# Edge rows of a graph layer: two chunks per load instead of one

## The chip, the cores and the metric

One Trainium2 chip, one core. The metric is the device time of one launch in microseconds (us). The kernel is one program with five instruction streams: TensorE (PE, with PEld for its weight loads), VectorE (DVE), ScalarE (ACT), GpSimd (POOL) and the queue of SyncE (SP), which does nothing here but wait and issue DMAs.

## The reference, cut to what matters

6,250 nodes of 128 features, 100,000 edges sorted by `dst`. Two graph layers follow one another.

```
# layer 0: messages by a small MLP, summed at dst, then node update and layer norm
h = silu(concat(x[src], x[dst], radial(edge_weight)) @ Wm1 + bm1)
h = silu(h @ Wm2 + bm2);  messages = h @ Wm3 + bm3
x = layernorm(x + node_mlp(x, segment_sum(messages, dst)))
# layer 1: every edge's 128 attributes (edge_attr_128) are read once
xt   = logmap0(x)
att  = sigmoid(concat(xt[src], xt[dst], edge_attr) @ att_w.T + att_b)
sup  = xt + segment_sum(xt[src]*att, src) + segment_mean(edge_attr, src) + segment_mean(edge_attr, dst)
x = layernorm(x + proj(expmap0(sup)))
```

## The kernel before, in words

The edges are cut into 196 chunks of 512 (the last one overlaps its neighbour, so that it is full). All loops run over chunks in "ticks" that are written out: in each tick every engine does one step of several chunks at different depths.

**Layer 0** (ticks t = -6 to 218, `layer_*`). POOL gathers the source rows of a chunk with four indirect DMAs (L1069), PE, ACT and DVE form the messages (L1293 to L1333).

**Rows.** Layer 1 reads each chunk's attributes as a row buffer `row[i % 8]` of 128 partitions x 4 x 131 words; there are eight. The row tick r is t - 190, so rows begin while layer 0 ends; from r = 29 on the functions are `rest_*`. For row chunk i:

- SP loads it in tick i - 3: `row_load`, L890 to L897, one DMA of 256 KB. From i = 8 on it first waits until the four scatters of chunk i - 8 have landed (semaphore `sc`) and PE has read that buffer (`rp`).
- DVE (`rows_dve`) builds a one-hot (L978), multiplies the row with the attention weights (L981), and from chunk 62 on multiplies looked-up terms (L987) and copies one column (L989); ACT (`rows_act`) sums them (L944 up to chunk 61, L949 and L952 after it) and writes two columns of the row.
- POOL (`rows_pool`) scatters the row with four indirect DMAs (L933) into a table in HBM, sorted by source block.
- PE (`rows_pe`, L1010) adds the row into the sum at `dst`.

**Looks.** From chunk 62 on DVE needs a table look-up for the chunk: SP loads three small pieces in tick i - 4 (`look_load`, L1437, the last one is `bval`), DVE compares them (L1534) in tick i - 2, PE multiplies (L1639).

**Units.** The scattered table is read back in 206 units (`unit_load`, L1423), each one a one-hot on DVE (L1543), up to six matmuls on PE (L1660) and an addition on DVE (L1568). A unit of a group may only be loaded once the last chunk of that group has been scattered; seven buffers are used in turn.

In a tick of `rest_sp` the order on SP's queue is fixed: the row load of chunk r + 3, the look of chunk r + 4, then the units of tick r + 2. Whatever SP waits for, all behind it waits too.

```
for r in RTICKS:
    batch_sp(e, R0 + r)
    ...
    rows_sp(e, r)
    if C1 <= r + 4 < M:
        look_load(r + 4)
    for k in UTICK.get(r + 2, []):
        if unit_at(k) is not None:
            unit_load(unit_at(k))
```

**The end.** After the last rows (tick 195) PE runs the units of ticks 196 to 198, then transposes the sum at `dst` (L1648, with ACT L1492 between), then the last 25 units, and DVE and ACT finish the nodes.

Of the kernel before, what the change touches and what calls it, by code (L numbers as in the profile page):

```python
# [2 lines left out]
N, E, H = 6250, 100000, 128  # L3
P = 128
NB = 49
NP = NB * P
ME = 512
M = 196
# [9 lines left out]
NE, NGP, NOD = 8, 6, 4  # L18
# [3 lines left out]
RC = H + 3  # L22
# [10 lines left out]
def edge0(m):  # L33
    return min(m * ME, LASTB)
# [155 lines left out]
def gnn_kernel(nc, A, out):  # L190
# [6 lines left out]
    V, S, T, G, SP = nc.vector, nc.scalar, nc.tensor, nc.gpsimd, nc.sync  # L197
# [3 lines left out]
    with ctx:  # L201
# [7 lines left out]
        def region(name, size):  # L209
            return Region(sb(name, [P, size]), size)  # L210

        def take(reg, shape, dt=f32):
            n = 1
            for k in shape:
                n *= k
            return reg.take(shape, None if dt == f32 else dt, n // 2 if dt == bf16 else n)

        s = {n: ctx.enter_context(nc.semaphore(n)) for n in PRO + LAYER + NODES + ROWS + REST}
# [49 lines left out]
        ring = region("ring", 17408)  # L268
# [448 lines left out]
        od2 = [take(ring, [4, W]) for _ in range(NO2)]  # L717
        prod = [take(ring, [4, H + W]) for _ in range(NPR)]
        bwin = [take(ring, [W]) for _ in range(NWN)]
        row = [take(ring, [4, RC]) for _ in range(NE)]  # L720
        assert ring.off >= STAGE + 13 * 4 * H
        pat = take(ring, [FILL * RC])
        lgs = [take(ring, [4]) for _ in range(2)]
# [19 lines left out]
        def small_free(e, t):  # L743

            e.wait_ge(s["acch"], min(M, t - 8))
            e.wait_ge(s["tot"], min(M, t - 2))
            e.wait_ge(s["cnt"], min(M, t - 2))
            e.wait_ge(s["acce"], min(M, t - R0 - 2))
# [137 lines left out]
        def look(e, name, i):  # L886

            if i >= C1:
                e.wait_ge(lk[name], M + i - C1 + 1)

        def row_load(e, i):
            e0 = edge0(i)
            if i >= NE:
                e.wait_ge(s[f"sc{i % NE}"], 64 * (i // NE))
                e.wait_ge(s["rp"], i - NE + 1)
            SP.dma_start(row[i % NE][:, :, 0:H], A["edge_attr_128"][e0:e0 + ME, :].rearrange(
                "(s p) f -> p s f", p=P)).then_inc(s[f"ea{i % NE}"], 16)  # L897

        def window_load(e, i):
            e.wait_ge(s["abw"], 48)  # L900
            e.wait_ge(s["dm"], i - NWN + 1)
            SP.dma_start(bwin[i % NWN], btab[bass.ds(window(SP, i), W)].rearrange("(o w) -> o w", o=1).to_broadcast(
                [P, W])).then_inc(s[f"wn{i % NWN}"], 16)

        def rows_loaded(e, i):

            for j in range(NE):
                if i >= j:
                    e.wait_ge(s[f"ea{j}"], 16 * ((i - j) // NE + 1))

# [8 lines left out]
                    e.wait_ge(s[f"sc{j}"], 64 * ((i - j) // NE + 1))  # L919

        def rows_sp(e, r):
            if 0 <= r + 3 < M:
                row_load(e, r + 3)
            if 0 <= r + 3 < C1:
                window_load(e, r + 3)
# [10 lines left out]

        def rows_act(e, i):
            if 0 <= i < M:
                e.wait_ge(s[f"ea{i % NE}"], 16 * (i // NE + 1))
                S.copy(row[i % NE][:, :, RC - 1:RC], lo["s"][:, :, i:i + 1])  # L940
                e.wait_ge(s["dm"], i + 1)
                if i < C1:
                    for n in range(4):
                        k = S.activation(prod[i % NPR][:, n, :], prod[i % NPR][:, n, :], ACT.Identity,  # L944
                                         accum_out=row[i % NE][:, n, H:H + 1])
                    k.then_inc(s["lb"], 1)
                else:
                    for n in range(4):
                        k = S.activation(prl[i % NPR][:, n, :], prl[i % NPR][:, n, :], ACT.Identity, accum_out=lgs[i % 2][:, n:n + 1])  # L949
                    k.then_inc(lk["dot"], 1)  # L950
                    look(e, "dot", i)
                    S.activation(row[i % NE][:, :, H:H + 1], lgs[i % 2].rearrange("p (s o) -> p s o", o=1), ACT.Sigmoid,  # L952
                                 bias=attb[:, :]).then_inc(s["lb"], 1)

        def row_bank(i):

            return small_bank(R0 + i + 1) if i < RL - 1 else banks[(3, 7, 4)[i % 3]]
# [14 lines left out]
        def rows_dve(e, r):  # L972
            i = r
            if 0 <= i < M:
                v = prod[i % NPR] if i < C1 else prl[i % NPR]
                e.wait_ge(s["lb"], i - NPR + 1)
                e.wait_ge(s["rp"], i - NO2 + 1)
                V.tensor_tensor(od2[i % NO2], iotap[:, 0:W].rearrange("p (o b) -> p o b", o=1).to_broadcast([P, 4, W]),  # L978
                                rel[:, :, i:i + 1].to_broadcast([P, 4, W]), ALU.is_equal).then_inc(s["odr"], 1)
                e.wait_ge(s[f"ea{i % NE}"], 16 * (i // NE + 1))  # L980
                V.tensor_tensor(v[:, :, 0:H], row[i % NE][:, :, 0:H], attp.rearrange("p (o f) -> p o f", o=1).to_broadcast(  # L981
                    [P, 4, H]), ALU.mult)
                if i >= C1:
                    bk = banks[(1, 2)[i % 2]][:, :].rearrange("p (s m) -> p s m", s=4)
                    look(e, "prd", i)
                    for n in range(4):
                        V.scalar_tensor_tensor(out=v[:, n, H:H + NM], in0=iota[:, 0:NM], scalar=srcm[:, n, i:i + 1], in1=bk[:, n, 0:NM],  # L987
                                               op0=ALU.is_equal, op1=ALU.mult)
                    V.tensor_copy(v[:, :, H + NM:H + NM + 1], bk[:, :, NM:NM + 1]).then_inc(s["dm"], 1)  # L989
                    return  # L990
                e.wait_ge(s[f"wn{i % NWN}"], 16 * (i // NWN + 1))
                e.wait_ge(s["dm"], i)
                V.tensor_copy(bwinp, bwin[i % NWN]).then_inc(s["bwp"], 1)
                e.wait_ge(s["odr"], i + 1)
                e.wait_ge(s["bwp"], i + 1)
                V.tensor_tensor(v[:, :, H:H + W], od2[i % NO2], bwinp.rearrange("p (o b) -> p o b", o=1).to_broadcast([P, 4, W]),  # L996
                                ALU.mult).then_inc(s["dm"], 1)

        def rows_pe(e, r, first):
            i = r - 1  # L1000
            if 0 <= i < M:
                bk = row_bank(i)
                if i < RL - 1:
                    small_free(e, R0 + r)
                else:
                    e.wait_ge(s["acce"], max(i - 2, RL - 1))
                e.wait_ge(s["odr"], i + 1)
                e.wait_ge(s[f"ea{i % NE}"], 16 * (i // NE + 1))
                for n in range(4):
                    k = T.matmul(bk[:, 256:256 + W], row[i % NE][:, n, 0:H], od2[i % NO2][:, n, :], start=(first and n == 0),  # L1010
                                 stop=(n == 3), skip_group_check=True)
                k.then_inc(s["rp"], 1)
# [62 lines left out]
        def layer_act(e):  # L1075
            settled(e)
            for t in TICKS:
# [32 lines left out]
                if j is not None:  # L1110
                    e.wait_ge(s["nz"], j + 1)
                    e.wait_ge(s["n1"], j)
                    S.activation(nu[:, 0:n, :], nz[:, 0:n, :], ACT.Silu).then_inc(s["nu"], 1)
                batch_act(e, t)
                rows_act(e, t - R0)

        def ranks_ready(e):
# [47 lines left out]
        def layer_dve(e):  # L1165
# [4 lines left out]
            for t in TICKS:  # L1170
# [101 lines left out]
                if j is not None:  # L1272
# [6 lines left out]
                    k.then_inc(s["nz"], 1)  # L1279
                batch_dve(e, c, t)  # L1280
                rows_dve(e, t - R0)

        def layer_pe(e):
# [131 lines left out]
        def rest_sp(e):  # L1415
# [23 lines left out]
            for r in RTICKS:  # L1439
                batch_sp(e, R0 + r)  # L1440
                if r == TAB:
                    e.wait_ge(s["abw"], 80)
                    e.wait_ge(s["pat"], 3)
                    for v in tw:
                        SP.dma_start(v[0:NQ, 0:NM], atab[0:N].rearrange("(q m) -> q m", m=NM)).then_inc(s["abb"], 16)
# [6 lines that stand above are left out]
# [243 lines left out]
        def early_done(e):  # L1695

            slots_done(e, RE - 1)
            rows_loaded(e, RL + 2)
            windows_loaded(e, RL + 2)
            e.wait_ge(s["rp"], RL - 1)  # L1700
            e.wait_ge(s["acce"], RL - 2)
            e.wait_ge(s["lb"], RL)
            e.wait_ge(s["odr"], RL)
            e.wait_ge(s["abw"], 48)
            e.wait_ge(s["zacc"], ZACC)
            e.wait_ge(s["mvs"], 2 * NB)
            e.wait_ge(s["zf"], 16 * len(FILLS))
# [413 lines left out]
```

## Time and profile before

| | us |
|---|---|
| three runs | 2115.41, 2115.46, 2117.05 (median 2115.46) |
| the profiled execution | 2115.82 |
| its span | 2114.0 |
| POOL busy | 1501.2 (71%) |
| DVE busy | 1693.4 (80%) |
| PE busy | 1550.7 (73%) |
| ACT busy | 1358.8 (64%) |

Busy times are sums over the whole span; what counts is which engine never waits in a stage, and which wait ends last. Of the 2115.82 us the span is 2114.0, so 1.8 us lie around it.

### The profile page before, as it was taken

The numbers are of one execution on the slowest core, as the hardware profiler recorded it, in microseconds if no ns is written. First come the engines' busy times: TensorE is split into PE (matmuls) and PEld (weight loads), VectorE is DVE, ScalarE is ACT, GpSimd is POOL, SyncE is SP. The second block draws the span as 40 slices with busy tenths as digits, with TensorE's granted clock in tenths as the row PEclk, the third lists the DMA queues.
The fourth block names the chain that finished last, engine by engine and source line by source line (L and its number), as shares of the span: only waits on it lengthen the run. The fifth ranks groups of instructions, "written<-read, shape, count | busy, mean of one in ns | idle before, by whom it ended". The sixth has DMA issues, their size and how long they took to land.

```text
span 2114.0 us, 41847 instructions
## 1 busy us (share of the span) xinstructions
PE 1550.7 (73%) x11127; PEld 1334.6 (63%) x11225; DVE 1693.4 (80%) x5532; ACT 1358.8 (64%) x3965; POOL 1501.2 (71%) x1572
## 2 busy tenths in 40 slices
PE   7787888888888887887874334676778877778850
PEld 7566666666676666666664334666677877778740
DVE  6877788788888888888766543899998788888887
ACT  4887787777787877987654533688884434434424
POOL 3777777777777777777777777777777777777700
PEclk9899999999999999999965555699999899989985
DMA  9577767676653434335464344788877778888822
GB/s 243 150 181 152 178 168 173 155 174 161 160 122 100 106 105 106 100 95 128 114 174 111 112 119 121 203 231 234 230 214 224 215 225 228 233 232 241 264 72 61
DMA packets 345860, 349.60 MB, mean 165 GB/s; under 512 B 67792, under 2 KB 273610, under 8 KB 345617
## 3 DMA queue, kind: packets, MB, share of 16 engines
q1 hardware_dynamic: 292193, 241.07, 44.5%
q0 software_dynamic: 50176, 104.07, 16.7%
q10 hardware_dynamic: 3248, 1.71, 0.3%
q8 instruction: 94, 1.54, 0.3%
q14 instruction: 149, 1.22, 0.2%
HBM read 249.43 MB, written 94.46 MB: 163 GB/s over the span
## 4 chain that ended last, share of the span: by engine, by line
DVE 36%; POOL 28%; issue 14%; DVEq 7%; PE 7%; ACT 3%; DMA 2%; SPq 1%; POOLq 0%; ACTq 0%
POOL gtab L933 20%; POOL ra L1069 9%; DVEq L758 7%; DVE ring L1193 4%; DVE ring L1203 3%; DVE rt L987 2%; DVE ring L1208 2%; DVE bank L1217 2%; DVE ring L1198 2%; DVE ring L1214 2%; PE bank L1660 2%; DVE ring L1195 2%; DVE ring L1543 1%; DVE ra L1178 1%; DVE ring L978 1%
## 5 line engine op out<-in xcount | busy, mean ns | idle before, releaser
L1069 POOL DMA_INDIRECT ra<-ptab,gis x784 | 746.8, 953 | 271.8 <-issue 225.8
L933 POOL DMA_INDIRECT gtab<-ring,idx x784 | 754.2, 962 | 239.1 <-issue 236.4
L949 ACT ACTIVATE rt<-rt 128x254 f32<-128x254 f32 x536 | 215.3, 403 | 291.2 <-DVE rt L989 291.2
L1010 PE MATMUL bank<-ring 128*128 128x78 f32 x1568 | 261.1, 323 | 127.5 <-DMA ring<-in_edge_attr 88.4
L1010 PEld LDWEIGHTS bank<-ring 128*128 128x128 f32 x1568 | 247.8, 241 | 137.9 <-issue 109.2
L1293 PEld LDWEIGHTS bank<-ring 128*128 128x128 f32 x1568 | 197.9, 195 | 143.7 <-DVE ra L1178 127.3
L1293 PE MATMUL bank<-ring 128*128 128x78 f32 x1568 | 209.7, 278 | 62.5 <-DVE ring L1185 56.0
L1660 PE MATMUL bank<-ring 128*128 128x130 f32 x1374 | 195.1, 293 | 57.1 <-DVE ra L1568 41.3
L1639 PE MATMUL bank<-rt 128*128 128x126 f32 x1072 | 165.8, 304 | 80.8 <-DVE rt L989 66.7
L1320 PE MATMUL bank<-wm,ring 128*128 128x128 f32 x1568 | 215.9, 283 | 10.8 <-ACT ring L1102 4.8
L1320 PEld LDWEIGHTS bank<-wm,ring 128*128 128x128 f32 x1568 | 213.5, 198 | 11.5 <-ACT ring L1102 5.6
L1660 PEld LDWEIGHTS bank<-ring 128*128 128x128 f32 x1374 | 174.6, 201 | 67.4 <-DVE ra L1568 47.7
L1639 PEld LDWEIGHTS bank<-rt 128*128 128x128 f32 x1072 | 149.2, 215 | 90.9 <-issue 90.9
L1082 ACT ACTIVATE ring<-bank 128x512 f32<-128x512 f32 x196 | 116.2, 593 | 137.8 <-PE bank L1320 136.1
L944 ACT ACTIVATE ring<-ring 128x206 f32<-128x206 f32 x248 | 89.6, 363 | 127.0 <-DVE ring L996 126.8
L1329 PE MATMUL bank<-cst,ra 128*128 128x128 f32 x784 | 127.1, 287 | 50.6 <-DMA ra<-ptab,gis 50.2
L1178 DVE TENSOR_TENSOR ra<-ra,bank 128x78 f32 x196 | 46.3, 236 | 131.8 <-issue 124.0
L1333 PE MATMUL bank<-ra,ring 128*128 128x512 f32 x264 | 148.0, 643 | 4.6 <-DVE ra L1252 3.8
L987 DVE SCALAR_TENSOR_TENSOR rt<-cst,rt,bank 128x125 f32<-128x125 f32 x536 | 147.3, 336 | 0.0
L1102 ACT ACTIVATE ring<-bank,bcol 128x512 f32<-128x512 f32 x196 | 134.7, 687 | 13.2 <-PE bank L1333 9.7
L1534 DVE TENSOR_SCALAR rt<-rt,cst 128x512 f32<-128x512 bf16 x134 | 67.4, 503 | 85.4 <-DMA rt<-bval 83.7
L1193 DVE TENSOR_TENSOR ring<-bank,lo_d 128x512 bf16<-128x512 f32 x196 | 133.9, 683 | 0.0
(274 smaller groups left out, 3587.0 us busy)
## 6 DMA issues: line engine op xcount, KB each, us to landing
ring<-in_edge_attr SPq DMA_DIRECT2D x196, 256.0 KB, 3.7
ring<-gtab SPq DMA_DIRECT2D x89, 393.0 KB
gtab<-ring SPq DMA_DIRECT2D x41, 687.8 KB
ra<-in_edge_weight SPq DMA_DIRECT2D x132, 128.0 KB
ring<-gtab SPq DMA_DIRECT2D x49, 327.5 KB
ring<-reld SPq DMA_DIRECT2D x196, 78.0 KB
ring<-gtab SPq DMA_DIRECT2D x49, 262.0 KB
ra<-ptab,gis POOLq DMA_INDIRECT x784
```

The costliest lines, as they stand in the source:

```text
L758: return eng.value_load(baser[0:1, m:m + 1], min_val=0, max_val=TOP)
L933: G.indirect_dma_start(out=gtab[group_of(i)][:, :], out_offset=bass.IndirectOffsetOnAxis(ap=idx[:, n, i:i + 1], axis=0), in_=row[i % NE][: ...
L949: k = S.activation(prl[i % NPR][:, n, :], prl[i % NPR][:, n, :], ACT.Identity, accum_out=lgs[i % 2][:, n:n + 1])
L987: V.scalar_tensor_tensor(out=v[:, n, H:H + NM], in0=iota[:, 0:NM], scalar=srcm[:, n, i:i + 1], in1=bk[:, n, 0:NM], op0=ALU.is_equal, op1=A ...
L1010: k = T.matmul(bk[:, 256:256 + W], row[i % NE][:, n, 0:H], od2[i % NO2][:, n, :], start=(first and n == 0), stop=(n == 3), skip_group_chec ...
L1069: G.indirect_dma_start(out=gp[i % NGP][:, n, :], out_offset=None, in_=ptab[:, :], in_offset=bass.IndirectOffsetOnAxis(ap=gis[:, n, i:i + 1 ...
L1193: V.tensor_tensor(l, iotap.rearrange("p (o b) -> p o b", o=1).to_broadcast([P, 4, P]), lo["d"][:, :, i:i + 1].to_broadcast([P, 4, P]), ALU ...
L1293: k = T.matmul(small_bank(t)[:, 0:W], val[i % NVAL][:, n, :], ohd[i % NOD][:, n, :], start=(n == 0), stop=(n == 3), skip_group_check=True)
L1320: k = T.matmul(bk[:, n * P:(n + 1) * P], h1[i % 2][:, n * P:(n + 1) * P], wm2[:, :], start=False, stop=True, skip_group_check=True)
L1333: T.matmul(bk[:, :], qw[i % NQW], rad[i % NRD], start=False, stop=True, skip_group_check=True).then_inc(s["h1p"], 1)
L1639: k = T.matmul(banks[(1, 2)[i % 2]][:, n * P:n * P + NM + 1], lkf[i % 2][:, n * P:(n + 1) * P], tw[i % NLK][:, 0:NM + 1], start=(n == 0), ...
L1660: k = T.matmul(bk[:, j * (H + 2):(j + 1) * (H + 2)], coh1[(u - 4) % NCO][:, j * nk + n, :], ct[(u - 4) % NCT][:, j * nk + n, 0:H + 2], sta ...
```

## The change

Row buffers are taken in pairs: `duo[k]` holds 8 x 131 words per partition, and `row[2k]`, `row[2k + 1]` are its halves, so the layout in memory is the same. `row_load` is called in every second tick, for the even chunk i, and loads chunks i and i + 1 with one DMA of 512 KB on the semaphore of the even buffer. It waits for the scatters of chunks i - 8 and i - 7 and for PE's reading of chunk i - 7. The last two chunks (194 and 195) are loaded in the same call by two DMAs, each on its own semaphore. All who read a row wait through `row_here`. The number of buffers (eight), their users, the looks, the units and the scatters are as before.

```diff
-        row = [take(ring, [4, RC]) for _ in range(NE)]
+        duo = [take(ring, [8, RC]) for _ in range(NE // 2)]
+        row = [duo[i // 2][:, 4 * (i % 2):4 * (i % 2) + 4, :] for i in range(NE)]
...
         def row_load(e, i):
-            e0 = edge0(i)
             if i >= NE:
                 e.wait_ge(s[f"sc{i % NE}"], 64 * (i // NE))
-                e.wait_ge(s["rp"], i - NE + 1)
-            SP.dma_start(row[i % NE][:, :, 0:H], A["edge_attr_128"][e0:e0 + ME, :].rearrange(
-                "(s p) f -> p s f", p=P)).then_inc(s[f"ea{i % NE}"], 16)
+                e.wait_ge(s[f"sc{i % NE + 1}"], 64 * (i // NE))
+                e.wait_ge(s["rp"], i - NE + 2)
+            if i < M - 2:
+                SP.dma_start(duo[i % NE // 2][:, :, 0:H], A["edge_attr_128"][i * ME:(i + 2) * ME, :].rearrange(
+                    "(s p) f -> p s f", p=P)).then_inc(s[f"ea{i % NE}"], 16)
+            else:
+                for v in (i, i + 1):
+                    e0 = edge0(v)
+                    SP.dma_start(row[v % NE][:, :, 0:H], A["edge_attr_128"][e0:e0 + ME, :].rearrange(
+                        "(s p) f -> p s f", p=P)).then_inc(s[f"ea{v % NE}"], 16)
+
+        def row_here(e, i):
+
+            if i < M - 1:
+                e.wait_ge(s[f"ea{i % NE // 2 * 2}"], 16 * (i // NE + 1))
+            else:
+                e.wait_ge(s[f"ea{i % NE}"], 16)
...
         def rows_sp(e, r):
-            if 0 <= r + 3 < M:
+            if 0 <= r + 3 < M and (r + 3) % 2 == 0:
                 row_load(e, r + 3)
...
         def rows_act(e, i):
             if 0 <= i < M:
-                e.wait_ge(s[f"ea{i % NE}"], 16 * (i // NE + 1))
+                row_here(e, i)
```

`rows_dve` and `rows_pe` get the same line as `rows_act`.

## Rows read from the trace of the kernel before

**Rows 1.** The page: busy time by engine; the two costliest groups

```profile
PE 1550.7 (73%) x11127; PEld 1334.6 (63%) x11225; DVE 1693.4 (80%) x5532; ACT 1358.8 (64%) x3965; POOL 1501.2 (71%) x1572
...
L1069 POOL DMA_INDIRECT ra<-ptab,gis x784 | 746.8, 953 | 271.8 <-issue 225.8
L933 POOL DMA_INDIRECT gtab<-ring,idx x784 | 754.2, 962 | 239.1 <-issue 236.4
```

**Rows 2.** Line L933: ns min/median/max, first and last start; its idle time by releaser

```profile
L933 POOL DMA_INDIRECT gtab<-ring,idx x784: 954/958/1250, 1019.4 to 2011.4; - x196
...
  issue: 236.4, 775
  ACT ring L944: 2.1, 7
  ACT ring L952: 0.6, 2
```

**Rows 3.** Chain that ended last, from 1940 us on: start, us, what

```profile
1955.37 6.09 DMA gtab<-ring,idx
...
1964.44 0.41 SPq L896
...
1966.53 4.08 DMA rt<-bval
1970.64 0.48 DVE rt L1534
...
1985.91 4.59 PE bank L1660 x24
...
1991.35 9.75 PE bank L1660 x84
...
2001.63 11.46 ACT ra L1492 x44
...
2013.46 9.44 PE bank L1660 x84
...
2026.31 12.17 PE bank L1660 x78
```

**Rows 4.** Timeline of SP's queue, 1960 to 1990 us

```profile
1970.44 0.38 SPq L896 DMA_DIRECT2D ring<-in_edge_attr  x1
...
1972.50 0.32 SPq L1437 DMA_DIRECT2D rt<-bval  x1
...
1974.27 0.40 SPq L896 DMA_DIRECT2D ring<-in_edge_attr  x1
```

**Rows 5.** Timeline of DVE, 1969 to 1990 us

```profile
1975.66 0.48 DVE L1534 TENSOR_SCALAR rt<-rt,cst 128x512 f32<-128x512 bf16 x1
...
1982.89 0.68 DVE L981 TENSOR_TENSOR rt<-ring,bank 128x512 f32<-128x512 f32 x1
```

**Rows 6.** Waits: engine line, waited for, us in total, times, longest

```profile
SPq L896 <- DMA gtab<-ring,idx: 359.6, 163, 5.2
```

**Rows 7.** Line L896: issue ns, waiters, landing us min/median/max

```profile
L896 SPq DMA_DIRECT2D ring<-in_edge_attr x196: 378/389/1642, 979.9 to 1974.3; - x196
...
  PE bank L1010: 88.4, 29
  DVE ring L981: 39.9, 30
  ACT ring L940: 24.0, 22
...
DMA to landing us min/median/max: 2.7/3.7/6.6
```

**Rows 8.** Windows with counts: L952 and L933 to chunk 108, L944 and L933 to chunk 8

```profile
0.00:1555.90 1555.90, 15.18 (x47) 0.88 0.59 153
...
0.00:1566.10 1566.10, 415.04 (x432) 0.88 0.59 154
...
0.00:1056.90 1056.90, 13.72 (x72) 0.96 0.58 143
...
0.00:1059.80 1059.80, 30.77 (x32) 0.96 0.58 144
```

**Rows 9.** Windows: us, busy PE PEld DVE ACT POOL, granted clock, DMA share, GB/s

```profile
1700.00:1975.00 275.00, 216.29 (x1693) 208.49 (x1693) 231.65 (x666) 114.37 (x549) 208.83 (x218) 0.93 0.81 233
...
1985.00:1991.00 6.00, 5.09 (x31) 5.09 (x31) 4.53 (x9) 1.70 (x9) 4.68 (x5) 0.72 1.09 367
1991.00:2001.00 10.00, 10.00 (x89) 9.87 (x88) 9.13 (x16) 0.00 (x0) 7.66 (x8) 1.00 0.96 298
```

**Rows 10.** Timeline of the end: PE L1660 at two moments

```profile
1971.10 1.55 PE L1660 MATMUL bank<-ring,pos 128*128 128x130 f32 x12
...
1985.91 2.97 PE L1660 MATMUL bank<-ring,gis 128*128 128x130 f32 x12 [2.02 <-DVE ra L1568]
```

More of the change, by code:

```diff
@@ L905, in rows_loaded @@
         def rows_loaded(e, i):
-            for j in range(NE):
+            for j in range(0, NE, 2):
                 if i >= j:
@@ L979, in rows_dve @@
                                 rel[:, :, i:i + 1].to_broadcast([P, 4, W]), ALU.is_equal).then_inc(s["odr"], 1)
-                e.wait_ge(s[f"ea{i % NE}"], 16 * (i // NE + 1))
+                row_here(e, i)
                 V.tensor_tensor(v[:, :, 0:H], row[i % NE][:, :, 0:H], attp.rearrange("p (o f) -> p o f", o=1).to_broadcast(
@@ L1007, in rows_pe @@
                 e.wait_ge(s["odr"], i + 1)
-                e.wait_ge(s[f"ea{i % NE}"], 16 * (i // NE + 1))
+                row_here(e, i)
                 for n in range(4):
```

## The prediction

> **What bounds the kernel now.** I read the page first. By busy time DVE leads with 80% and POOL has 71% [rows 1], but the idle time of POOL's two groups is almost all "issue": a short gap after each indirect DMA. The lines of L933 say it outright: 784 scatters from 1019.4 to 2011.4 us, idle 236.4 us by issue (775 times, 0.305 us each) and 2.7 us by anything else [rows 2]. So POOL, once it scatters, never waits: 992.0 us between first and last start, over 783 intervals, is 1.267 us each, 5.07 us a chunk. Nothing in DVE, PE, ACT or SP can bring its last scatter earlier, and a delay elsewhere costs POOL nothing as long as each row is ready in time.
>
> The second view is the chain that ended last, read at its end [rows 3]. The reader is to see that it leaves POOL at 1955, 57 us before POOL's last scatter is issued. It goes: a scatter lands, SP issues a row load and the look behind it (L896, then `bval`), DVE L1534 starts at 1970.64 when `bval` has landed, DVE works through the last rows, PE runs units (L1660), ACT and PE transpose (11.46 us of ACT), PE runs the rest until 2038.5, and DVE and ACT finish. From 1985.9 on every piece follows the one before it. So two things set the time: POOL's pace, and **when the last rows get through DVE**, which hangs on SP's queue, which hangs on POOL's scatters. The third view, the waits of SP's queue, confirms the link: L896 waited 359.6 us in 163 waits for scatters to land [rows 6]. Row loads are not issued when there is time, but when a buffer comes free.
>
> **The change part by part.**
>
> 1. *97 row DMAs fewer.* Each took SP 0.389 us to issue [rows 7], 38 us in all, out of a queue that spends 359.6 us waiting in front of that very line. Worth nothing while SP waits. The readers' waits for odd rows fall away too; a few hundredths each on engines that are not POOL. Nothing.
>
> 2. *The row itself comes later.* PE, DVE and ACT waited 88.4, 39.9 and 24.0 us for rows [rows 7], none of it POOL. An even row now waits for chunk i - 7 instead of i - 8: 5.07 us. Its load is 512 KB; from the 2.7 to 6.6 us of the 256 KB one [rows 7] I take a microsecond more for the second half: 256 KB at 233 to 298 GB/s [rows 9] are 1.1 to 0.9 us, nothing at the least. What hides it is POOL's lead time, and it is thinnest at two places. At chunk 8, ACT has finished the row at 1056.9 (72 instructions of L944, eight a chunk, nine chunks) and POOL starts it just after 1059.8 (32 scatters done) [rows 8]: 2.9 us. But that row was loaded 25 us before DVE used it (eight rows were free at the start), so 6 us more in the load don't reach it. At chunk 108 (the 47th L952, done by 1555.9; POOL comes after 1566.1, 432 scatters done) it is 10 us [rows 8]. There the whole DVE phase moves with the loads: minus 6 to 7.5 us, 3 to 4 us are left. POOL goes on unhindered: cost 0.
>
> 3. *The look behind the row load.* This is the step that costs. In an odd tick SP now stands in front of the pair until chunk r - 4 has landed, where it used to need only r - 5; the look of chunk r + 4 and the units of tick r + 2 are queued behind it. In even ticks it waits for no scatter. In the steady part that moves DVE by a chunk against POOL and is covered by the same lead time. At the end it isn't. The last look, for chunk 195, is issued in tick 191, which is odd. Before, its row load (chunk 194) went out at 1970.44 and `bval` at 1972.50, 2.06 us behind [rows 4]; L1534 ran at 1975.66 [rows 5]. Afterwards SP waits for what the load of chunk 195 waited for, 1974.27 [rows 4]: 3.83 us later. It then issues two row DMAs where one stood: 0.45 us. `bval` goes out at 1974.27 + 2.06 + 0.45 = 1976.78. With the 4.08 us that `bval` took on the chain [rows 3] L1534 starts at 1980.86 instead of 1975.66: **5.2 us later**. Bounds: with the 3.16 us between `bval`'s issue and L1534 of that tick (1972.50 to 1975.66), 4.3 us. At POOL's mean pace of 5.07 us instead of the 3.83 of this execution, and with the extra microsecond of a second row ahead of it in the rings, 5.07 + 0.45 + 0.92 + 1.0 = 7.4 us. I take the value in between, as its terms are the nearest rows.
>
> The tick before does not undo this: the look of chunk 194 goes out in an even tick with no wait, so DVE is through with its tick by 1979 and stands at the one of chunk 195.
>
> 4. *From there to the end.* DVE needs 7.2 us from that L1534 to L981 of the last row (1982.89 [rows 5]); then everything is in a row as before [rows 3]. PE was busy for 10.00 of 10.00 us from 1991 to 2001 [rows 9], so nothing there swallows a late start. The last scatter, issued at 2011.4 [rows 2], is needed by the last units after 2013.46 [rows 3]; it was there in time and still is. So the 5.2 us arrive whole.
>
> Sum: 0 + 0 + 5.2 us on the profiled execution's 2115.82 us, 2121.0; that execution lies 0.36 us above the median of 2115.46, so 2120.7.
>
> At one point the Trainium skill speaks against this sum. The rows say that no transfer's size is waited for by POOL [rows 2]. "DMA: Bandwidth & Descriptors", section "Anatomy of one DMA", gives a DMA a fixed part of about 2.0 us beside bytes / 436 GB/s, and its rules for authors ask for larger ones; an estimate by it is 3.2 us for a pair where two loads take 5.2 us, which would make the change a gain. No run here shows it, and it is a rival below.
>
> **The rivals.**
>
> *The shift is swallowed (not slower).* Place: PE between 1985.9 and 1991. There PE was granted 0.72 of its clock on average against 1.00 after it [rows 9], and twelve matmuls of L1660 took 2.97 us where they took 1.55 before [rows 10], after PE had stood idle for 2.02 us. It is the lower of its two levels, 1.2 GHz, for part of the stretch. If PE falls idle elsewhere in the new order and runs this stretch at 2.4 GHz, two such groups give back up to 2.8 us: 2120.7 - 2.8 = 2117.9. With the lower bound of step 3, 4.3 - 2.8 = 1.5 us, 2117.0. It decides from 1 us given back. For it: the idle gap of 2.02 us hangs on DVE. Against: PE will stand idle longer before 1981 than it did, which speaks for the lower clock.
>
> *POOL runs dry near chunk 108.* If the phase moves by more than the 10 us of lead [rows 8], POOL waits for ACT, and its end moves by what is missing. Should the pair cost DVE two chunks of pace (10.1 us) and the upper terms of step 3 (0.45 + 0.92 + 1.0) besides, 12.5 us, then 2.5 us are missing; POOL's scatters are late by that, and the last look with them: 2120.7 + 2.5 = 2123.2, or 2125.4 with the upper bound of step 3. For it: DVE is busiest there. Against: step 2 leaves 3 to 4 us.
>
> *The DMA queues were what held DVE (faster).* If the fixed part of a load counted, fewer loads would bring rows and looks sooner; half of DVE's 39.9 us of waits for rows [rows 7] would go, 20 us: 2095. By the page above this is the rule's outcome. For it: the DMA engines are 81% busy from 1700 to 1975 [rows 9]. Against: POOL waits for none of it, and the last look cannot go out before chunk 187's scatter lands.
>
> **How the numbers follow.** A measurement of this kernel tells 0.2%, 4.2 us, from no change: slower begins at 2119.7. Forecast (4.3 to 7.4 us, 2119.8 to 2122.9): 0.57. Swallowed, 2115.5 to 2119.6: 0.32. POOL dry, 2123 to 2126: 0.05. Faster, near 2095: 0.06. Slower 0.62, same 0.32, faster 0.06. The range holds the forecast with its bounds, the swallowed case and most of the dry one: 2115.0 to 2126.0; left out are the faster case and the edges.
>
> **What would show it.** Right: L933 again from about 1019 to 2011 us without waits; 99 row DMAs in L896; L1534 of the last look 4.3 to 6 us later, waiting for `bval`; transposes starting near 2006 instead of 2001. Step 2 wrong: POOL idle behind L944 or L952. Step 4 wrong: the last L981 late, but L1660 after the transposes not. The forecast as a whole is wrong if the last L1534 is not late, or if POOL's first or last scatter has moved.

## The result and the profile after

The changed kernel takes 2125.5 us (2124.95 to 2127.94, 5 runs) against 2116.09 us of the kernel before: 1.0045 times as long (95% interval 1.0034 to 1.0057), 9.4 us. A second measurement of the same kernel (e9 below) gave 1.0034 (1.0022 to 1.0047), 7.2 us. It is slower, as forecast, and by more than the 5.2 us of the forecast; 2125.5 lies just inside the range (2115.0 to 2126.0) and above the forecast's own bounds (2119.8 to 2122.9). The profiled execution took 2127.94 us, the longest of its five, so the differences of this one trace run some 2 us above those of the medians.

POOL's scatters after the change (line L947, the view of [rows 2]):

```profile
L947 POOL DMA_INDIRECT gtab<-ring,idx x784: 952/958/1251, 1018.8 to 2014.7; - x196
its engine sat idle before it (us, times) until:
  issue: 226.8, 742
  ACT ring L966: 12.8, 38
  ACT ring L958: 1.7, 4
```

The reader is to see two things. The last scatter starts 3.3 us later, at 2014.7 instead of 2011.4. (The first one started 0.6 us earlier, but the second started at 1020.7 in both traces, so nothing was lost by that.) And ACT's L966, the last step of a row, is now named 38 times instead of twice. POOL's timeline around chunk 106 shows what that is, with the ACT line that released it:

```profile
1556.39 0.96 POOL L947 DMA_INDIRECT gtab<-ring,idx  x1 [0.30 <-issue]
1558.86 1.00 POOL L947 DMA_INDIRECT gtab<-ring,idx  x1 [1.50 <-ACT ring L966]
```
```profile
1557.80 0.30 ACT L966 ACTIVATE ring<-ring,attb 128x4 f32<-128x4 f32 x1
```

Instead of the usual 0.30 us POOL stood for 1.50 us, because the row was ready only at 1558.10. At chunk 8 it stood 0.81 us for L958:

```profile
1060.42 0.95 POOL L947 DMA_INDIRECT gtab<-ring,idx  x1 [0.81 <-ACT ring L958]
```

These two stops are 1.2 and 0.5 us of the 3.3. The other 1.6 us are in the scatters themselves, which were busy for more of the time than the 754.2 us of before [rows 1], and no wait goes with that:

```profile
L947 POOL DMA_INDIRECT gtab<-ring,idx x784 | 755.8, 964 | 241.4 <-issue 226.8
```

The end of the chain that ended last (the view of [rows 3]), as far as it stands in SP's queue and behind it:

```profile
1974.32 6.15 DMA gtab<-ring,idx
1980.53 0.38 SPq L903
1980.95 0.52 SPq L903
...
1983.83 3.69 DMA rt<-bval
1987.54 0.58 DVE rt L1548
...
1997.88 4.49 PE bank L1674 x24
...
2003.33 9.75 PE bank L1674 x84
...
2013.61 11.49 ACT ra L1506 x44
...
2025.48 9.44 PE bank L1674 x84
...
2038.33 12.18 PE bank L1674 x78
```

From the PE pieces on it is the same chain, link for link, 12 us later: the PE piece of 24 stands at 1997.88 (before 1985.91), the transposes' ACT piece at 2013.61 (before 2001.63), the last PE piece at 2038.33 (before 2026.31). Ahead of them it differs: before, the `bval` on the chain was that of chunk 194 [rows 3], here it is that of the last look. DVE's timeline, the last look and the last row:

```profile
1987.54 0.58 DVE L1548 TENSOR_SCALAR rt<-rt,cst 128x512 f32<-128x512 bf16 x1 [4.10 <-DMA rt<-bval]
...
1994.86 0.68 DVE L995 TENSOR_TENSOR rt<-ring,bank 128x512 f32<-128x512 f32 x1
```

DVE stood 4.10 us for `bval`; before it hadn't stood there at all [rows 5]. From the last row to the end of the span it is 2126.0 - 1994.86 = 131.1 us, and before it was 2114.0 - 1982.89 = 131.1 us [rows 5]. In seven of the traces below it is 130.9 to 131.1 us again, in e1 and e9 129.3, in e6 and e11 133.9 and 133.4. So in most traces what delays the last row delays the end by as much.

So one figure weighs each kernel below, **how far the last row runs ahead of POOL**: from L981 of chunk 195 (its line is another one in some kernels) to the start of the last scatter. Before it is 2011.4 - 1982.89 = 28.5 us [rows 2, 5], after it is 2014.7 - 1994.86 = 19.8 us. Of the 12 us of this trace 3.3 are POOL's and 8.7 the shrunken lead. Each such figure comes from one execution.

### The profile page after: what moved, and what is told of

Its sections match the earlier page's. It is cut to its first block, busy times and chain, and to the rows that moved or that the text cites. A ratio compares the mean times of both kernels' runs of the same rounds, so it can differ in the third digit from the quotient of the medians.

```text
span 2126.0 us, 41648 instructions
## 1 busy us (share of the span) xinstructions
PE 1547.9 (73%) x11127; PEld 1332.0 (63%) x11225; DVE 1688.9 (79%) x5532; ACT 1358.2 (64%) x3965; POOL 1503.3 (71%) x1572
## 4 chain that ended last, share of the span: by engine, by line
DVE 36%; POOL 23%; issue 14%; DMA 7%; DVEq 7%; PE 7%; ACT 4%; SPq 2%; POOLq 0%; ACTq 0%
POOL gtab L947 14%; POOL ra L1083 8%; DVEq L759 7%; DVE ring L1207 4%; DVE rt L1001 3%; DVE ring L1217 3%; DMA gtab<-ring,idx 3%; DMA rt<-bval 3%; DVE ring L1222 2%; DVE bank L1231 2%; PE bank L1674 2%; DVE ring L1212 2%; DVE ring L1228 2%; DVE ring L1209 2%; DVE rt L995 1%
## 5 line engine op out<-in xcount | busy, mean ns | idle before, releaser
L947 POOL DMA_INDIRECT gtab<-ring,idx x784 | 755.8, 964 | 241.4 <-issue 226.8
L958 ACT ACTIVATE ring<-ring 128x206 f32<-128x206 f32 x248 | 89.7, 363 | 93.6 <-DVE ring L1010 93.6
L1116 ACT ACTIVATE ring<-bank,bcol 128x512 f32<-128x512 f32 x196 | 134.8, 688 | 11.9 <-PE bank L1347 8.5
L1548 DVE TENSOR_SCALAR rt<-rt,cst 128x512 f32<-128x512 bf16 x134 | 66.8, 499 | 94.5 <-DMA rt<-bval 94.1
```

Source lines behind the costliest of these rows:

```text
L947: G.indirect_dma_start(out=gtab[group_of(i)][:, :], out_offset=bass.IndirectOffsetOnAxis(ap=idx[:, n, i:i + 1], axis=0), in_=row[i % NE][: ...
```

## The experiments

Theory: SP's queue makes look and units wait behind the pair, which costs at the end, and POOL's lead near chunks 8 and 106 is used up. Rival: the rows themselves come too late, or the transfer of 512 KB costs. All ratios are to the kernel before, measured beside it on the same chip, and the microseconds named with a ratio are worked out from it. e1 to e4 ran on one chip, where the kernel before stood at 2116.2 us, e5 to e8 and e9 to e11 on another, where it stood at 2120.1 and 2119.6, so only ratios are compared.

**e1, pairs up to chunk 167, and e2, pairs from chunk 168 on.**

```diff
+        def paired(i):
+            return 0 <= i < 168          # e2: 168 <= i < 194; e8: 64 <= i < 120
...
+            if paired(i):                # one load for i and i + 1, as in the change
+                if i % 2:
+                    return
+            else:                        # one load for i, as before the change
```

> Pairs up to chunk 167, single loads from 168 on. Theory (the late look at the end costs 5 to 7 us, POOL running dry near chunks 8 and 106 costs 2 to 3): the end is as before, POOL's last scatter stays 2 to 3 us late, so 2117.5 to 2119.5. Rival, only the end counts: 2116 (nothing left). Rival, all of it is POOL being late or slower scatter landings everywhere: 2121 or more.

> Single loads up to chunk 167, pairs from 168 on (194 and 195 singly, as before the change). Theory: the end's share alone, 5 to 7 us, POOL's scatters end at 2012 as before: 2121 to 2123. Rival, all from POOL: 2116. If both shares add up, this run's difference and that of e1 give the whole, 9 us.

e1: 2117.81 us, 1.0005 (0.9996 to 1.0014). e2: 2121.19 us, 1.0026 (1.0016 to 1.0035), 5.5 us. The end's share is real and the larger one; the pairs of the first 168 chunks cost 1.1 us, and their interval includes no change at all. Together the two make 6.6 us, against 7.2 to 9.4 for the whole. e2's queue shows something that the forecast had not in it (SP's timeline, where L908 is a pair and L915 a single load, then DVE's):

```profile
1965.33 0.40 SPq L908 DMA_DIRECT2D ring<-in_edge_attr  x1
...
1971.19 0.42 SPq L915 DMA_DIRECT2D ring<-in_edge_attr  x1
...
1973.42 0.32 SPq L1460 DMA_DIRECT2D rt<-bval  x1
```
```profile
1980.07 0.48 DVE L1557 TENSOR_SCALAR rt<-rt,cst 128x512 f32<-128x512 bf16 x1
...
1987.30 0.68 DVE L1004 TENSOR_TENSOR rt<-ring,bank 128x512 f32<-128x512 f32 x1
```

Chunks 194 and 195 are single loads there and wait singly, and the last `bval` went out at 1973.42, not late. Yet DVE came to the last look at 1980.07, with no wait in front of it: it was still busy with the ticks that the pair before (L908) had held up. In those ticks it had waited for `bval` in every second one (2.25 us at 1950.84, 1.01 at 1960.77, 0.79 at 1971.23). The delay isn't made by the last pair alone; it is DVE's whole phase, set by each pair in turn.

**e3, the waits of the change with two loads of 256 KB.**

```diff
-            if i < M - 2:
-                SP.dma_start(duo[i % NE // 2][:, :, 0:H], ...).then_inc(s[f"ea{i % NE}"], 16)
-            else:
-                for v in (i, i + 1):
+            for v in (i, i + 1):
...
         def row_here(e, i):
+            e.wait_ge(s[f"ea{i % NE}"], 16 * (i // NE + 1))
```

> The waits of the change, but each pair as two loads of 256 KB on two semaphores. Theory: the wait costs, not the size: 2124 to 2127, as after the change (0.45 us more of issue in front of the look). Rival, the 512 KB transfer itself costs (it lands later or delays scatters and looks): back by half or more, 2116 to 2120.

2123.09 us, 1.0032 (1.0020 to 1.0045). This is just under the 2124 to 2127 expected; most of the loss is there without a single large transfer. Against the first 1.0045 it left room for a share of the size, so it was repeated as e10.

**e4, the look ahead of the row load.** **e5, look and units ahead of it.**

```diff
-                rows_sp(e, r)
                 if C1 <= r + 4 < M:
                     look_load(r + 4)
+                rows_sp(e, r)            # e4: here
                 for k in UTICK.get(r + 2, []):
                     if unit_at(k) is not None:
                         unit_load(unit_at(k))
+                rows_sp(e, r)            # e5, e6: here instead
```

> The change, with the look issued ahead of the row load in SP's queue from tick 29 on. Theory: what the pair delays is the look behind it; freed of it, DVE is only held by the rows, which come 6 to 8 us earlier than DVE used them: 2111 to 2117. Rival, the late rows or the bigger transfer cost: 2121 to 2126.

e4: 2121.31 us, 1.0023 (1.0014 to 1.0032). The theory in this form missed: the loss did not go. It is smaller than that of the change (1.0045 and 1.0034), but the interval overlaps with that of e9. The chain and DVE's timeline of e4 say why:

```profile
1978.28 5.50 DMA ring<-gtab
```
```profile
1983.80 0.96 DVE L1557 TENSOR_TENSOR ring<-bank,ring 128x768 f32<-128x768 f32 x1 [2.21 <-DMA ring<-gtab]
```

The look (L1548 in this kernel) no longer waits behind the pair, and the unit load, next behind it, does. So the next kernel freed both.

> The change, with look and units both ahead of the row load in SP's queue from tick 29 on. Theory now: all that is queued behind the pair's wait comes late, and with the look freed it was the unit load (DVE waited 2.2 us for it in tick 193 of e4); with both freed DVE is held by its own work: 2112 to 2117. Rival, the late rows themselves or their size: 2121 as in e4.

e5: 2119.35 us, 0.9998 (0.9989 to 1.0007): the loss is gone, with every pair, its late rows and its 512 KB transfers in place. In its trace, which is of its fastest execution (2116.03 us), the last look and last row on DVE stand where they stood before the change (1975.66 and 1982.89 [rows 5]):

```profile
1975.74 0.51 DVE L1548 TENSOR_SCALAR rt<-rt,cst 128x512 f32<-128x512 bf16 x1
...
1983.00 0.68 DVE L995 TENSOR_TENSOR rt<-ring,bank 128x512 f32<-128x512 f32 x1
```

POOL's scatters run from 1019.1 to 2011.1 us in it, 992.0 us, as in the kernel before.

**e6, the same order with single loads.** The edit is e5's on the kernel before.

> The kernel before, with the same order on SP's queue: look, units, row load. Theory: the wait for a scatter stood in front of both before the change too, so this is faster than before, by 1 to 4 us: 2112 to 2115; and the pairs of e5 cost little against it, 0 to 3 us. Rival, DVE at the end is held by the rows: 2116, no change.

2117.17 us, 0.9987 (0.9978 to 0.9997). It was repeated as e11. This kernel, and not the one before, has the same order as e5: between the two, pairs cost 2.2 us by the medians (2119.35 against 2117.17), and the two intervals overlap.

**e7, single loads on time, look and units late.**

```diff
                 rows_sp(e, r)
+                if (r + 3) % 2 == 0 and r + 3 < M:
+                    e.wait_ge(s[f"sc{(r + 4) % NE}"], 64 * ((r + 4) // NE))
                 if C1 <= r + 4 < M:
                     look_load(r + 4)
```

> The kernel before with its single row loads at their old times, but with a wait for the scatter of chunk r - 4 put between row load and look in odd ticks of the rest stage. Theory: look and units are as late as with pairs, rows are not: the most of the change's loss, 2121 to 2125, with the last look 5 us late or more and POOL's lead near chunk 106 used up. Rival, the late or bigger row load is the cause: 2116.

2124.33 us, 1.0023 (1.0014 to 1.0032), 4.9 us. This is the counterpart to e5: the row loads and their waits are those of the kernel before, and the loss is of the size of the end's share (e2). Its chain, then DVE's timeline:

```profile
1974.81 5.11 DMA gtab<-ring,idx
...
1981.54 4.23 DMA rt<-bval
```
```profile
1985.80 0.49 DVE L1536 TENSOR_SCALAR rt<-rt,cst 128x512 f32<-128x512 bf16 x1 [1.70 <-DMA rt<-bval]
...
1993.03 0.69 DVE L981 TENSOR_TENSOR rt<-ring,bank 128x512 f32<-128x512 f32 x1
```

One part of the expectation missed. The row was ready 2.1 us ahead of POOL's scatter at chunk 106, not at the least value of 0.76 us, so POOL didn't run dry, and this kernel lacks that share. It also stays below the 7.2 us of the whole.

**e8, pairs for chunks 64 to 119 alone** (the edit of e1).

> Pairs for chunks 64 to 119 alone. Theory: POOL's lead near chunk 106 goes from 5.9 to its least value, 0.8 us, POOL's last scatter is 0 to 1.5 us later, the ramp is as before; the phase is back by the end, so 2116 to 2118. Rival, the loss of e1 came from the ramp: lead of 2 us or more left, 2116.

2120.64 us, 1.0001 (0.9992 to 1.0010). POOL's timeline has the same stop, before the same scatter of chunk 106:

```profile
1561.57 1.00 POOL L956 DMA_INDIRECT gtab<-ring,idx  x1 [1.50 <-ACT ring L975]
```

So the pairs of this stretch make POOL run dry, as the theory said; that it costs time can't be told from the runs of this kernel. In e1, whose pairs cover this stretch too, the row of chunk 106 was just in time (0.8 us ahead) and POOL made no stop before the same scatter:

```profile
1556.74 0.96 POOL L956 DMA_INDIRECT gtab<-ring,idx  x1 [0.31 <-issue]
```

**e9, the change again; e10, e3 again; e11, e6 again.**

> The changed kernel once more, to weigh its parts on one chip: the end's share (5.5 us in e2) and POOL's (1 to 2 us in e1 and e8) make 6.5 to 7.5 us, so a ratio near 1.0033. If it is 1.0045 again, some 2.5 us are not in these two parts. The last row (its L981) should stand 7 to 9 us nearer to POOL's last scatter than in the kernel before.

> The waits of the change with two loads of 256 KB, beside e9 on the same chip. Theory: size costs nothing, the same as e9 within 2 us. Rival: the 512 KB load is worth 2 to 3 us against it, as 2125.5 against 2123.1 us of the first runs seemed to say.

> The order of e6 (look, units, row load; single loads) again: 0.9987 again, 2 to 4 us faster than before. With e5 (0.9998) it leaves 2 us for the pairs themselves where neither look nor unit waits behind them. If it is 1.0, e6 was chance.

e9: 2126.78 us, 1.0034 (1.0022 to 1.0047). e10: 2126.15 us, 1.0029 (1.0017 to 1.0041). e11: 2118.27 us, 0.9995 (0.9986 to 1.0004). The size of the load makes no difference that can be seen: 1.0034 and 1.0029 on one chip. The trace of e9 is a second one of the changed kernel, and its last ticks went another way (DVE's timeline, then windows with columns as in [rows 9]):

```profile
1986.36 0.43 DVE L1582 TENSOR_TENSOR ra<-ra,bank 128x260 f32<-128x260 f32 x1 [1.03 <-PE bank L1674]
...
1987.35 0.48 DVE L1548 TENSOR_SCALAR rt<-rt,cst 128x512 f32<-128x512 bf16 x1
```
```profile
1982.00:1988.00 6.00, 6.00 (x39) 6.00 (x39) 4.57 (x13) 2.08 (x10) 4.75 (x5) 0.69 0.93 282
...
1997.00:2003.00 6.00, 5.40 (x48) 5.40 (x49) 5.48 (x11) 1.38 (x7) 4.66 (x5) 1.00 0.74 212
```

The last `bval` went out at 1982.28, 9.8 us later than before the change, but DVE came to the last look at 1987.35 with no wait for it; just ahead it had waited for PE, which ran at 0.69 of its clock on average. Behind the last row PE had its full clock, and the tail was 129.3 us. So the late phase stands in both traces, but which wait ends last in the last tick does not repeat.

e11 doesn't confirm e6; together they say a microsecond or two faster at best, and that row last with single loads beats the kernel before is not shown.

All kernels by the two causes. "Scatters" is the time from the first to the last start of a scatter, "dry" whether POOL stopped at chunk 106, "lead" the figure defined above:

| kernel | ratio | scatters us | dry | lead us |
|---|---|---|---|---|
| before | 1 | 992.0 | no | 28.5 |
| after; e9 | 1.0045; 1.0034 | 995.9; 995.3 | yes | 19.8; 20.2 |
| e3; e10 | 1.0032; 1.0029 | 994.9; 995.5 | yes | 21.1; 19.8 |
| e1, pairs to 167 | 1.0005 | 995.0 | no, just in time | 26.8 |
| e2, pairs from 168 | 1.0026 | 993.4 | no | 23.5 |
| e8, pairs 64 to 119 | 1.0001 | 995.4 | yes | 27.9 |
| e7, late look | 1.0023 | 993.2 | no | 22.3 |
| e4, look first | 1.0023 | 993.9 | no | 24.9 |
| e5, row last | 0.9998 | 992.0 | no | 28.1 |
| e6; e11, singles, row last | 0.9987; 0.9995 | 993.7; 994.8 | no | 33.2; 31.7 |

The five traces with a dry POOL have 995.4 us on average, the eight without 993.5. As those without lie anywhere from 992.0 to 995.0, the averages don't give the price of running dry; the stop itself is 1.2 us long. With a lead of 24.9 us or less a kernel is slow (1.0023 or more), with 26.8 or more it isn't. e6 and e11 gained 3 to 5 us of lead, but their last rows stand at 1982.0 and 1983.0, no more than 0.9 us earlier than before; it is POOL's last scatter that was later in these traces. From their last row to the end it is 2115.9 - 1982.0 = 133.9 and 2116.4 - 1983.0 = 133.4 us instead of 131.1. Their chains say what the end waited for (e6's):

```profile
1979.76 2.66 DMA gtab<-ring,idx
...
1982.43 3.75 DMA ring<-gtab
...
1987.55 4.89 PE bank L1660 x24
```

A scatter lands, the unit load that waited for it goes out, and PE starts the units at 1987.55, 1.6 us later than before although the last row was earlier. e11's chain has the same two transfers. So once the look and the last rows are early enough, the unit loads behind POOL's scatters set the end. No kernel was run to test this.

## Why the prediction was right, and where it fell short

*What bounds the kernel, and step 3: right.* The view that carried the forecast was the chain leaving POOL at 1955 us (56 us before the last scatter, not 57) and running through SP's queue to a look, that of chunk 194, and through DVE's last rows to PE. e5 and e7 take the cause apart: late rows with look and units ahead of them cost nothing against the kernel before, and against the same order with single loads 2.2 us by the medians (e6), which is not clear of noise; late look and units with rows on time cost 4.9 us. This agrees with the Trainium skill, "DMA: Bandwidth & Descriptors", section "Anatomy of one DMA": a wait on a semaphore is done by the issuing sequencer before it dispatches, not by the DMA engines. Here whatever is next on that sequencer stands too, as e4 and e5 show.

*The number: inside the range by the room left for a rival.* The step summed to 2120.7 us with bounds up to 2122.9, and the kernel took 2125.5. That is where the forecast put "POOL runs dry", with a chance of 0.05; only the room for it makes 2125.5 fall into the range. The repetition's 7.2 us would be 2122.7 on the same base, inside the bounds. By its own signs the forecast missed as well: the last look was to be 4.3 to 6 us late and was 11.9, the transposes were to start near 2006 and did near 2013, and POOL's last scatter, which was not to move, moved by 3.3 us.

*Step 3's size: too small.* The sum was a wait of 3.83 us more, 0.45 us for the second issue, and the difference of the landings. In the trace after, the row load of chunk 194 went out at 1980.53 instead of 1970.44 [rows 4], 10.1 us later. Of these 5.1 are one chunk of POOL's pace (3.83 was the value of one execution with uneven landings; 5.07 stood in the upper bound). POOL's own lateness is 3.5 at this point: the last scatter of chunk 187 started at 1974.32 (the chain above), and before at

```profile
1970.77 1.19 POOL L933 DMA_INDIRECT gtab<-ring,idx  x1 [0.30 <-issue]
```

The rest, 1.5, is a scatter's landing: the load went out 6.2 us after the start of the scatter it waited for, where the load of chunk 194 before went out 4.7 us after its own (1965.72 in POOL's timeline). The landings are uneven: the load of chunk 195 before went out 3.5 us after that of 1970.77, so the 3.83 us that the forecast took from these two loads hid 1.2 us of a chunk's pace. `bval` followed the load by 3.30 us instead of 2.06, and DVE started 3.7 us after `bval`'s issue instead of 3.16. Together 11.9 us for the last look of this trace, where 5.2 were forecast and 7.4 was the bound. The medians say 7.2 to 9.4 us in all, of which e2 shows 5.5 at the end.

*Step 3, "the tick before does not undo this": incomplete.* I looked at one late look. e2 shows that DVE's phase is late before it and that DVE did not catch up in the last ticks, and in e9 it stood before the last look without waiting for `bval`. e4 shows that the units behind the pair hold DVE as well, which the forecast named as queued there and gave no price.

*Step 2, "POOL goes on unhindered: cost 0": wrong, by a misread row.* POOL's lead time near chunk 108, which is how long a row is ready before POOL starts on it, was taken as 10 us from counting 47 instructions of L952 up to 1555.9 us [rows 8]. The view of that line in the kernel before has two kinds:

```profile
L952 ACT ACTIVATE ring<-ring,attb x134: 301/302/307, 1315.0 to 1986.4; 128x4 f32<-128x4 f32 x134
L952 ACT ACT_TABLE_LOAD  x1: 1283/1283/1283, 1313.7 to 1313.7; - x1
```

One of the 47 is a table load, so the 47th belonged to chunk 107. Chunk 108 is the next one, which in ACT's timeline of before is

```profile
1560.03 0.30 ACT L952 ACTIVATE ring<-ring,attb 128x4 f32<-128x4 f32 x1
```

and ends at 1560.33, 5.9 us before POOL's scatter at 1566.2, not 10. In the trace after the figure is 0.8 us from chunk 106 on, the least that any of the traces has, and POOL stands. The step's own shift of 6 to 7.5 us was right: at chunk 105 this lead time was 8.4 us and is 2.0. With the right figure for chunk 108 this shift uses up the lead and gives the rival "POOL runs dry near chunk 108" the upper hand: it happened, at chunk 106. The stop there cost POOL 1.2 us, less than the 2.5 us that the rival named. So the cost that step 2 put at nothing was real, and the 3.3 us of POOL's lateness in this trace are more than the stop (see above).

*Chunk 8.* The forecast said that 25 us between load and use keep the ramp, the ticks in which rows begin while layer 0 still runs, out of it. POOL stood at chunk 8 for 0.7 to 0.9 us in six of the seven traces with pairs, or their waits, in the ramp (not in e5), and in one of the six without them (e11). It is at the edge; pairs seem to push it over, but that they are the cause isn't shown, as no kernel paired these chunks alone.

*Step 4, "the 5.2 us arrive whole": right for the first trace, nearly so for the second.* It is 131.1 us from the last row to the end before, after and in e5. In the first trace the rival in which PE swallows the shift by running at its higher clock did not come: PE was granted 0.72 of its clock for six microseconds again, just 12 us later (windows of the trace after, columns as in [rows 9]):

```profile
1997.00:2003.00 6.00, 5.12 (x31) 5.12 (x32) 4.94 (x10) 1.67 (x9) 4.75 (x5) 0.72 0.65 194
```

In e9, the same kernel, it did come in part: 1.00 in this stretch, as shown there, and a tail shorter by 1.8 us. But the low clock of that trace lay a few microseconds ahead instead, where it held DVE before the last look. The forecast gave this rival 0.32; its mechanism exists, and it did not keep the kernel from being slower.

*The rival "the DMA queues held DVE":* fell. Larger loads (e9) and loads of the old size with the same waits (e10) cost the same, and e5, with 97 loads fewer and neither look nor unit behind them, is level with the kernel before. DVE's waits for rows, which this rival wanted to halve, grew from 39.9 us [rows 7] to 63.4 in the trace after (line L995):

```profile
  DMA ring<-in_edge_attr: 63.4, 18
```

No run here shows a fixed cost of a load on the path that sets the time. The figures that the forecast took from the Trainium skill, "DMA: Bandwidth & Descriptors", section "Anatomy of one DMA", are fitted there to DMAs issued by GpSimd, and these loads are issued by SP: by that fit, an estimate, 256 KB take 2.6 us, and here they landed after 3.7 us in the median [rows 7].

## What to carry to other kernels

Joining two loads joins their waits: the pair goes out when the later buffer is free, and everything behind it in that queue waits with it, so price the instructions behind the load and not the load. If a load must wait for a buffer, put it last in its tick, behind the loads that don't: here this took away the loss of the pairs, while a gain with single loads isn't shown. And before counting instructions of a line to find an iteration, look at the kinds in it: one table load shifted the count here and turned a lead of 6 us into 10.

## What the runs showed of the hardware that was not expected

The kernel before had medians of 2116.2 us on one chip and of 2120.1 and 2119.6 on another, with single runs from 2112.24 to 2123.67 us. POOL's indirect DMAs differ between executions too. A scatter's median is 958 ns in the traces before, after and in e4, e5, e9 and e10, 959 in e1, e2 and e3, and 962 in e6, e7, e8 and e11, with the least one at 957 there instead of 952 to 954 ns. Over 784 scatters 4 ns are 3 us, as much as a good part of the effects looked for here. All four with 962 ns ran on the chip of e5 to e11 and have no pairs, or pairs in 56 chunks alone (e8); the three on that chip with the paired waits throughout have 958. On the chip of e1 to e4 there is no such gap: e2, single for 168 chunks, has 959, and the kernels with more pairs have 958 or 959; on which chip before and after ran is not on record. What makes the difference is open, and as the kernel before has no trace from the chip of e5 to e11, so is how much of the chips' difference it is. Small differences of this kernel can only be told by ratios over many executions side by side.
